# Attention stage of a six-stage transformer kernel: other engines and an earlier step for the queries, and its end handed to the next stage

## The reference, cut to what matters

```python
qkv = (x @ Wqkv.T + bqkv).reshape(B, S, 3, H, d).transpose(2, 0, 3, 1, 4)   # H = 16 heads, d = 8
kb = kp[:, :, idx, :]                      # keys of a window, padded by 32 on both sides
scores = jnp.einsum('bhncd,bhnld->bhncl', qc, kb) / np.sqrt(d)
scores = jnp.where(band, scores, -jnp.inf)
attn = jax.nn.softmax(scores, axis=-1)
o = jnp.einsum('bhncl,bhnld->bhncd', attn, vb)
return o @ Wout.T + bout
x = x + L1_attn_ref(layernorm(x), ...)
x = x + 0.5 * L1_ffn_ref(layernorm(x), ...)
```

## Time and profile before

| | |
|---|---|
| median of 3 runs | 1823.41 us (1822.92 to 1826.37) |
| the profiled execution | 1829.28 us |
| its span in the profile | 1827.5 us |
| TensorE busy | 1630.0 us, 89% |
| VectorE busy | 1258.8 us, 69% |
| ScalarE busy | 1076.7 us, 59% |
| GpSimd busy | 1196.7 us, 65% |
| attention block in the trace | about 1333 to 1606 us |

### The profile page before, as it was taken

How to read it: one execution, slowest core, us unless ns; L and a number is a source line. 1 busy time by engine, 2 the same in 40 slices (tenths; PEclk the granted TensorE clock), 3 DMA queues, 4 the chain that set the end, 5 groups by cost and what they waited for, 6 DMA issues and landing times. The chain is left out here.

```text
span 1827.5 us, 40267 instructions
## 1 busy us (share of the span) xinstructions
PE 1630.0 (89%) x14217; PEld 1396.1 (76%) x14217; DVE 1258.8 (69%) x2948; ACT 1076.7 (59%) x1947; POOL 1196.7 (65%) x1191
## 2 busy tenths in 40 slices
PE   6999898999999989988687998999968888889998
PEld 6888777777778867876566897788857777778887
DVE  2359889788898887888989435544456877656443
ACT  3476766766667757666665545344357777743442
POOL 4238787786877867879898534466556576544663
PEclk9999999999999999998898999999979999989999
DMA  5023333333333323322232311111346665311113
GB/s 154 1 73 114 102 98 101 96 96 99 112 96 108 101 82 114 96 96 85 86 97 64 105 52 35 35 49 47 116 137 184 187 184 175 95 34 37 49 51 105
DMA packets 141089, 171.23 MB, mean 94 GB/s; under 512 B 32246, under 2 KB 76316, under 8 KB 140892
## 3 DMA queue, kind: packets, MB, share of 16 engines
q1 hardware_dynamic: 133852, 153.06, 27.9%
q0 software_dynamic: 7040, 15.60, 2.7%
HBM read 116.30 MB, written 52.30 MB: 92 GB/s over the span
## 5 line engine op out<-in xcount | busy, mean ns | idle before, releaser
L833 POOL TENSOR_TENSOR db<-du_m,bt 128x512 f32<-128x512 f32 x256 | 329.1, 1287 | 116.9 <-DVE bank L838 116.2
L838 DVE TENSOR_TENSOR_SCAN bank<-bank,db 128x512 f32<-128x512 f32 x256 | 312.7, 1221 | 18.2 <-ACT bank L823 17.6
L864 POOL TENSOR_TENSOR y_m<-y_m,ph 128x512 f32<-128x512 f32 x240 | 312.8, 1304 | 2.0 <-DVE ph L853 2.0
L823 ACT ACTIVATE bank<-dt_m,a_neg 128x512 f32<-128x512 f32 x256 | 176.3, 689 | 86.0 <-DVE ph L853 79.1
L853 DVE TENSOR_TENSOR ph<-bank,ct 128x512 f32<-128x512 f32 x240 | 166.0, 692 | 9.4 <-POOL y_m L864 1.0
L1368 POOL TENSOR_TENSOR s_a<-s_a,mx_a 128x768 f32<-128x768 f32 x64 | 94.0, 1469 | 65.1 <-DVE mx_a L1459 61.1
L1445 PE MATMUL bank<-kT_a,qd_a 128*128 128x96 f32 x512 | 76.7, 295 | 38.3 <-ACT qd_a L1269 36.3
L1445 PEld LDWEIGHTS bank<-kT_a,qd_a 128*128 128x128 f32 x512 | 67.2, 203 | 47.0 <-ACT qd_a L1269 40.4
L375 PEld LDWEIGHTS bank<-dn,hf1b 128*128 128x128 f32 x680 | 90.2, 194 | 16.2 <-DVE x_all L437 6.8
L375 PEld LDWEIGHTS bank<-dn,hf2b 128*128 128x128 f32 x680 | 90.1, 194 | 15.9 <-DVE x_all L437 8.3
L375 PEld LDWEIGHTS bank<-dn,hf0b 128*128 128x128 f32 x688 | 90.3, 193 | 12.0 <-DVE x_all L437 2.8
(11 more groups left out here) (474 smaller groups left out, 4723.9 us busy)
## 6 DMA issues: line engine op xcount, KB each, us to landing
bt<-bc_rows SPq DMA_DIRECT2D x128, 256.0 KB, 3.5
ct<-bc_rows SPq DMA_DIRECT2D x128, 256.0 KB, 3.4
sorted<-zero_row SPq DMA_DIRECT2D x64, 288.0 KB, 4.0
kT_a<-k_rows SPq DMA_DIRECT2D x32, 256.0 KB, 3.4
q_strips_a<-q_rows SPq DMA_DIRECT2D x32, 256.0 KB, 4.3
q_rows<-q_hi_a SPq DMA_DIRECT2D x16, 256.0 KB
q_rows<-q_lo_a SPq DMA_DIRECT2D x16, 256.0 KB
k_rows<-k_hi_a SPq DMA_DIRECT2D x16, 256.0 KB, 3.4
```

Source lines behind the costliest of these rows:

```text
L823: eng.activation(DH[J % 2][:], dt[s % 2][:, j % NH, :], ACT.Exp, scale=a_neg[:, j % NH, j // NH:j // NH + 1]).then_inc(da_done.sem)
L833: eng.tensor_tensor(db[J % RD][:], du[s % 2][:, j % NH, :], bt[N % RB][:], ALU.mult).then_inc(db_done.sem)
L838: eng.tensor_tensor_scan(DH[J % 2][:], DH[J % 2][:], db[J % RD][:], 0.0, ALU.mult, ALU.add).then_inc(hs_done.sem)
L864: eng.tensor_tensor(y[s % 2][:, j % NH, :], y[s % 2][:, j % NH, :], ph[J % RP][:], ALU.add).then_inc(ys_done.sem)
```

## The change

- `attention`: ScalarE sets one head of a group (head 0, in step 2n-5, and now in front of `copy_out` and `copy_p`), GpSimd sets three (head 1 in step 2n-6, heads 2 and 3 in step 2n-5).
- The preparation of the next sequence, its stores and first strips, the projection and the norms' means and roots all stand one step earlier. Where the next sequence's `load_out` and `store_values` stand (k=2) does not change.
- The queries of groups 0 and 1 are set in the stage in front: group 0 by ScalarE behind its last `shared_act`, group 1 by VectorE (`set_next`). The second `clear_group` goes there too, `bias_out(0)` comes from there into the attention. Tiles are laid at other addresses to make this possible.
- Two one-element activations load ScalarE's tables for Exp and Gelu earlier.
- The last `load_out` and projection and the norm of sequence 7 go into the last stage (`closing`); the 28 matmuls of `warm` are gone.

```diff
@@ attention
-        q_set, q_set2 = S.count("a_queries_set", NG, (0, 1)), S.count("a_queries_set_pool", NG, (2, 3))
+        q_set, q_set2 = S.count("a_queries_set", NG, (0,)), S.count("a_queries_set_pool", NG, (1, 2, 3))
-                copy(dst, src).then_inc(q_set.sem if r < 2 else q_set2.sem)
+                copy(dst, src).then_inc(q_set.sem if r < 1 else q_set2.sem)
+        def set_next(eng):
+            eng.wait_ge(q_set.sem, q_set.at(0, 0))
+            eng.wait_ge(q_set2.sem, q_set2.at(0, 3))
+            set_queries(eng, eng.tensor_copy, 1, range(HG))
@@ attention, sync
-            load_values(eng, 0)
             strips(eng, 0, 2)
             strips(eng, 0, 3)
+            load_values(eng, 0)
-                if k == (0 if s >= 1 else 1) and more:
-                    store_queries(eng, s + 1)
-                    store_keys(eng, s + 1)
-                    strips(eng, s + 1, 0)
+                ahead_of = s + 1 if k < GU - 1 else s + 2
+                if (t == 1 or t >= GU - 1 and k == GU - 1) and ahead_of < NSEQ:
+                    store_queries(eng, ahead_of)
+                    store_keys(eng, ahead_of)
+                    strips(eng, ahead_of, 0)
-            load_out(eng, NSEQ - 1)
@@ attention, pool
-            clear_group(eng, 1)
-            set_queries(eng, eng.tensor_copy, 1, (2, 3))
                 if t == 0:
-                    set_by_pool(eng, 2, 2, 2)
-                n, r = ((t + 5) // 2, 2) if t % 2 else (t // 2 + 2, 3)
+                    set_by_pool(eng, 2, (1, 2, 3), 2)
+                n = (t + 6) // 2
                 if n < NG:
-                    set_by_pool(eng, n, r, t + 2)
+                    set_by_pool(eng, n, (2, 3) if t % 2 else (1,), t + 2)
@@ attention, prepared and projected
-            names = {(0, 0): "T", (1, 0): "q", (1, 2): "k", (2, 0): "v"} if t < 3 else {(6, 2): "T", (7, 0): "q", (7, 2): "k", (1, 0): "v"}
+            names = {(0, 0): "T", (1, 0): "q", (1, 2): "k", (2, 0): "v"} if t < 3 else {(5, 2): "T", (6, 0): "q", (6, 2): "k", (1, 0): "v"}
-            return (s,) if t % GU == 5 and 0 <= s < NSEQ - 1 else ()
+            return (s,) if t % GU == 4 and 0 <= s < NSEQ - 1 else ()
@@ attention, pe
-            warm(eng, BT[0], K["up_hi"][0], 20)
-            project_pe(eng, NSEQ - 1)
-            warm(eng, BT[0], K["up_hi"][0], 4)
@@ attention, act
-            set_queries(eng, eng.copy, 1, (0, 1))
+            eng.activation(table[:], C["one"][:], ACT.Exp)
                 if t + 1 < NU:
                     exps(eng, t + 1)
+                n = (t + 6) // 2
+                if t % 2 and n < NG:
+                    set_queries(eng, eng.copy, n, (0,))
...
-                n, r = ((t + 5) // 2, 0) if t % 2 else (t // 2 + 2, 1)
-                if n < NG:
-                    set_queries(eng, eng.copy, n, (r,))
                 if t == NU - 2:
+                    eng.activation(table[:], C["one"][:], ACT.Gelu)
@@ ffn1 (last stage): sync, pool, pe, dve
+            if closing:
+                closing["load_out"](eng, NSEQ - 1)
+                if s == 1 and not first:
+                    norms.root(eng, NSEQ - 1)
+                if v == 1 and closing:
+                    closing["project_pe"](eng, NSEQ - 1, HT[1].psum)
+                if v == 2 and closing:
+                    closing["project_dve"](eng, NSEQ - 1, HT[1].psum)
+                    eng.wait_ge(*closing["projected"])
+                    norms.mean(eng, NSEQ - 1)
@@ ffn1 (stage in front): act, dve
-                if opening and J >= AJ - 1:
-                    opening["set_queries"](eng, eng.copy, 0, (0, 1))
-                opening["set_queries"](eng, eng.copy, 0, (2, 3))
+                opening["set_queries"](eng, eng.copy, 0, range(4))
+                if opening and J == AJ:
+                    opening["set_next"](eng)
```

More of the change, by code:

```diff
@@ L1070, in front, with attention @@
             block.tensor(pe)
-def attention(nc, S, C, bank, K, a, host):
+def attention(nc, S, C, bank, K, a, host, closing):
     NB = SEQ // QB
@@ L1081, in attention @@
     GD = HG * HD
-    RQ, RS, RK = 3, 3, 4
+    RQ, RS, RK, HOLE, GAP = 3, 3, 4, UB * KW + 3 * P, 3 * P
     AHEAD, RZ = 3, 4
@@ L1276, in clear_group @@
         def clear_group(eng, r):
-            for t in (kT[r],) + ((kT[RQ],) if r == RQ - 1 else ()):
+            for t in (kT[0:2], (), kT[2:])[r]:
                 eng.memset(t[:, 0:PAD].bitcast(F32), 0.0)
@@ L1564, in act @@
                         copy_p(eng, t, 1)
-                    if place == 2 and k == 5 and s + 2 < NSEQ:
+                    if place == 2 and k == 4 and s + 2 < NSEQ:
                         norm_out(eng, s + 2)
@@ L1791, in pool @@
                 K["pool"](eng, tri_f)
-            else:
-                norms.root(eng, NSEQ - 1)
             if opening:
@@ L2171, in dve @@
             for v in SLOTS:
-                if v == -2:
+                if v == -2 and first:
                     norms.mean(eng, NSEQ - 1)
-                if v == 1:
+                if v == (1 if first else 5):
                     norms.scale(eng, NSEQ - 1)
@@ L2270, in program @@
         front(nc, S, C, bank, sb, a["L0_attn_x"], a, f0, K, f1, M["sorted"])
-        last = ffn1(nc, S, C, bank, K, M, "_f1b", out, None, True)
-        stage = attention(nc, S, C, bank, K, a, last)
+        closing = {}
+        last = ffn1(nc, S, C, bank, K, M, "_f1b", out, None, True, closing)
+        stage = attention(nc, S, C, bank, K, a, last, closing)
         every(ffn1(nc, S, C, bank, K, M, "_f1", None, next(stage)))
```

75 lines of the change are left out of this document (40 added, 35 removed).

## The result

| | before | changed |
|---|---|---|
| first measurement, median (20 runs each) | 1826.51 us (1817.14 to 1836.02) | 1814.88 us (1804.55 to 1828.52) |
| ratio, 95% interval | | 0.9935 (0.9915 to 0.9954) |
| the same two kernels, second measurement (x5) | 1881.12 us | 1863.20 us, 0.9897 (0.9866 to 0.9928) |
| third (x13) | 1828.26 us | 1815.99 us, 0.9923 (0.9896 to 0.9949) |
| profiled execution: time, span, clock | 1829.3, 1827.5, 0.966 | 1819.4, 1817.3, 0.963 |

Faster, by more than the 0.2% that can be told. The direction was right, the size was not; the median lies just inside the upper end of the range (1816).

A forecast was written before the change was run, and what follows sets the result against it. TensorE's 34.0 us of waits for ScalarE's query casts bound the kernel, with the DRAM path nearly as long as a round. Rounds -12.3, rest -4.5, start -2, end -4: -22.8; 1829.3 - 22.8 - 5.9 (offset) gives 1801 us, range 1786 to 1816.

The forecast's parts named there:

- Both DMA waits: In the rounds: TensorE waits some 2 us at the projection for the outputs' load, ScalarE before `norm_out` for the values' store.
- The rounds at full clock: Attention's five rounds: 29.2 us each, between 27.9 and 29.9; with 0.4 for low clock 29.6 against 32.05, giving -12.3 us.
- The start: Start of the attention block: fifth scores about 1.4 us sooner, 0.6 from group 1 set in front; -2 us.
- The end: Last copy to next stage: gap -6.3 us, table load -1.3, some 3.6 given back; -4 us together.
- The small term for VectorE's k_shift: Seven VectorE instructions may each wait for a GpSimd cast, at most 4 us against the change; taken as zero.
- I add 0.4 for the low clock: In each round: 0.4 us for slow clock where 1.5 was read before, most of it falling into idle time.
- the rest of the block: Attention outside the rounds and start: 5.9 us of TensorE's query waits and some more after 1570 us go; -4.5 us.
- The reason named for the round's bound: In the rounds: SyncE's queue does not get shorter, so landings of outputs and values bound a round at 29.2 us.
- Rival 1: In the rounds: engines are the bound and the DRAM path hides; rounds of 27.0 us, 1786 us; chance 0.17.
- Rival 2: At the last stage's start: without the fillers the clock is already down; +4.5 us, 1805.5 us; chance 0.12.
- Rival 3: At the scores: GpSimd's third head or strips' wait holds TensorE instead; rounds of 31.5 us, 1813.6 us; chance 0.12.
- Rival 4: In the rounds: late landings are paid one after another; rounds of 34.2 us, 1828 us; chance 0.07.

The follow-up runs named there:

- x8: The kernel before with only the changed casts (ScalarE one head, GpSimd three, one step further ahead); preparation, stores and end as before; ratio 0.9960 to the kernel before.
- x2: The kernel before with only the joined end and the Gelu table loaded ahead; ratio 0.9989 to the kernel before, interval 0.9965 to 1.0012.
- x11: The changed kernel with SyncE's store of the values ahead of the load of the outputs; ratio 0.9889 to the kernel before, 6 runs.
- x10: The changed kernel with the projection and its add half a step later, no fillers; ratio 0.9948 to the kernel before.
- x18: x16 with SyncE's store of the values ahead of the load of the outputs; ratio 0.9881 to the kernel before, 1807.30 us.
- x16: The changed kernel with x9's late cast and filler matmuls at the strips' wait, block start, projections and joined end; ratio 0.9891 to the kernel before, 1810.45 us.
- x17: x16 measured once more, unchanged; ratio 0.9907 to the kernel before.
- x9: The changed kernel with ScalarE's cast of the first group of sequence 1 behind its step's copies again; ratio 0.9947 to the kernel before.
- x3: The changed kernel with two heads cast by ScalarE and two by GpSimd, ScalarE casting in every step, still one step further ahead; ratio 1.0000 to the kernel before.

## Why the prediction was right or wrong

**Right.** TensorE's waits for ScalarE's casts went, all 34.0 us. Both DMA waits came at the places named. Ahead of `norm_out` they are 1.7 to 3.0 us. At the projection, where some 2 us a round were forecast, they are 0.2, 0.6, 2.0 and 2.3, and three times none. The rounds at full clock: 29.2 was forecast, 29.2, 29.3 and 29.3 are read. That they agree so well is in part luck: 29.2 was picked between 27.9 and 29.9, and of the 14.2 us that TensorE is idle in the five rounds only 2.8 are waits for the outputs and 4.4 for ScalarE's copy of xT; 5.4 are nine short waits for VectorE ahead of the turn of the outputs, which the forecast did not have. The start: from the first scores to the fifth 12.0 us in place of 13.8, -1.8 where 1.4 of the -2 were meant. (The other 0.6 lie ahead of the first scores, where x8, whose stage in front is the old one, is as short as the change; they are not shown.) The end: gap 6.2 shorter for the 6.3, and given back 1.9 in the last stage, so -4.3 for -4 in the first batch and 3 to 4 in the slower ones; x2's times give 2. The small term for VectorE's k_shift stayed small: its seven instances take 3.1 us in all (before, most took 1.2 each), and no wait of TensorE in the rounds names GpSimd.

**Wrong: "I add 0.4 for the low clock ... most of which now falls into idle time".** This is the term that failed. The rounds lost 4.7, 8.2 and 6.8 us in three traces, 1.3 us a round and not 0.4, since TensorE is busy 136 of 150 us: little idle time is left for a slow stretch to hide in. With it the rounds gave -9.9, -5.5 and -6.7, a mean of -7.4, for the forecast -12.3.

**Wrong: the rest of the block, -4.5.** I counted waits that go and no clock. The mean of the three blocks is 257.8, 7.5 less than before; less the rounds and the start, the rest is +1.7. Outside the rounds 18.0, 18.6 and 16.4 us were lost, in the kernel before 11.1: 6.6 more. Without it the rest would be -4.9, close to the forecast. Most of the increase stands at a wait that is not new, the one for the strips of sequence 1: between the second and the third query matmul 3.3 us were lost before (5.6 in x2) and 5.6, 10.0 and 7.8 in the change, although TensorE's longest wait there is about the same, 3.7 us before and 3.6, 4.8 and 3.5 after. The rest of it is in the steps behind the rounds, 0.0 before and 7.0, 1.7 and 1.7 after, where the 7.0 stand behind the late outputs. The prediction read of the clock only that a window had 0.94 and that the last stage's start had 0.66; it never asked what stood in front of each fall, which would have shown that every one follows idle time of TensorE, and that a new wait of 2 us can cost more than its length.

**Wrong, small: the offset.** I took 1823.4 as the level of the kernel before; 20 runs have 1826.5. 3 us of the miss against 1801 are this.

**The reason named for the round's bound** was half right. SyncE's chain does make both waits. But x11 took the values' wait away and x10 the outputs', and neither shortened the round in its trace (29.6 us at full clock in both): each time the next landing, or TensorE's own 136.19 / 5 = 27.2 us with its small waits, stood behind it. No single chain is shown to be the bound. With the values first and all waits filled (x18) a round is 29.0 in place of 29.4 and 29.2 (x16, x17), so that a small gain from it remains possible.

**The rivals.** Rival 1 (27.0) did not come. Rival 2 (the clock without the fillers) came in part: 0.72 in the first 15 us of the last stage for 0.66 before, nothing more lost in the first batch, and 1 to 6 us more lost than with the old end in the slower ones, of which 2 to 3 show in the stage's length. Rival 3 did not: no wait for GpSimd's casts in the rounds. Rival 4, waits in a row, came at one place of the changed kernel (1362.88, where it cost what the strips would have cost anyway, x9), and in full in x3.

**What stays open.** Why a fall lasts 3 us in one execution and 14 in the next at the same place, and so why the strips' wait costs the changed kernel more; what the joined end is worth in time, where the traces say 3 to 4 us and the runs can't tell; how much time a given loss costs, since less came back with fillers than the runs of one kernel suggest; and why both kernels took some 50 us longer in the routed stages of two batches.

## What to carry to other kernels

Where TensorE is over 85% busy, price a wait by what the clock does behind it: look at every fall of the granted clock and at the wait in front of it, and count most of the slow stretch, since little idle time is left to hide it. Give the work that waits for a DMA to the engine with nothing urgent behind it: with GpSimd taking the early casts their new places were worth 7 us (x8), with ScalarE casting in every step the whole gain of the change was gone (x3). Fillers in such waits lifted the clock in these runs, but gave back less time than clock; below about 10 us compare many runs, not two profiles.

## What had not been expected

- TensorE's granted clock fell some 100 times in 20 blocks, every time behind 0.9 to 3.4 us of idle TensorE, and the loss in one kernel's block ranged from 22.7 to 26.8 us between executions.
- The rest of the block at full clock repeats within 1.1 us in the changed kernel (234.3, 233.3, 233.2), far better than its length (257.0, 260.1, 256.4): a better measure of a change than the time of one execution.
- 9.5 of the 10.4 us that the change takes out of the block at full clock come with the new places of the casts alone; the new start and the whole preparation a step earlier gave about 1 together.
- The mean granted clock went from 0.966 to 0.975 with fillers and the time from 1816.0 to 1810.5, less than half of what runs of one kernel show for such a difference, and with intervals that overlap.
